# Routing and expert networks in one program block, with lists that carry three numbers for each token

## The chip, the cores and the metric

The kernel runs on one core of one Trainium2 chip. The metric is the device time of one execution in microseconds (us), the median of several runs. The engines are TensorE (PE; its weight loads are PEld), VectorE (DVE), ScalarE (ACT), GpSimd (POOL) and SyncE (SP), which here only issues DMAs. An engine works through its own queue in order; engines wait for each other by semaphores.

## What is computed

A sequence of 16 x 512 tokens with 512 features goes through an attention layer (16 heads, one shared key and value head) and then through a mixture of 16 experts in which each expert picks its 512 tokens. The second half is what the change touches:

```
xn     = xf / rms * norm_weight                      # 8192 tokens x 512
logits = xn @ router_weight.T + router_bias          # 8192 x 16
probs  = softmax(logits)
_, idx = top_k(logits.T, 512)                        # each expert: its 512 best tokens
h      = gelu(xn[idx] @ fc1.T + fc1_bias)            # 2048 hidden
y      = h @ fc2.T + fc2_bias
output = scatter_add(y * gates); divided by the sum of a token's gates
return x + output
```

Matrix products are done in three passes of single precision parts (hi x hi, hi x lo, lo x hi) in the format fp32r.

## The kernel before

It has these stages, each a block of its own, in which every engine has its own program; between two blocks all engines meet.

1. `make_lists`: constants and the list of attention tile pairs.
2. `attend` (0 to about 527 us): a software pipeline over tile pairs. `turn` in each engine's program sets the order of its steps. At the end DVE runs `logits_elsewhere` (L916, L919), which fills in the logits of token tiles that are equal to a common one.
3. A block that clears the 125 semaphores of `attend`, so that their numbers can be used again: SP, POOL, ACT and DVE clear 31 or 32 each.
4. `route` (530 to 616 us): the logits (64 tiles of 128 tokens x 16 experts) are brought into the form 128 rows x 1024, where 8 rows belong to one expert. A search of 16 rounds finds each expert's 512th largest value. In a round ACT and DVE count how many values reach four limits, PE adds the counts, DVE takes the next limits. The softmax is done beside the rounds. Then DVE ranks the chosen tokens (two scans, L1515 and L1518), adds the two kinds of rank (L1528), PE turns the result back to tiles (`b_pos`), and DVE makes from it `pos_f` (the place of each token in each expert's list, L1541), gates divided by their sums (L1548), and two digits of each place, `pos_a` and `pos_b` (L1553 to L1557). SP writes `meta` (gates, and the row of `xn_dram` where the token's features are: 32 numbers, 128 bytes, for each token) to `meta_dram`.
5. `experts` (616 us to the end). For each expert n, DVE builds two sets of flags from the digits (`hot`: `hot_a`, L1908; `named`, L1913 to L1923), PE sums 64 small matmuls into a list of 512 token numbers (`make_list`, L2054, into the PSUM bank `b_turn`), DVE turns that into integers (`name`, L1928 and L1932), POOL moves the list so that it has one number for each partition (`move_list`, L1716), fetches the rows of `meta_dram` (`fetch_meta`, L1722) and with the origin numbers in them the rows of `xn_dram` (`fetch_rows`, L1737). PE turns the rows (L2063), ACT and DVE split them and their sums into hi and lo (`x_hi`, `x_lo`). Then come 8 periods for each expert: 7 products of fc1 in a scheme of Strassen's kind (L2074) and 24 matmuls of fc2 (L272 to L274). POOL makes the weight sums for fc1 (`weight_sums`, L1706 to L1711), ACT and DVE split weights. SP loads weights two buffers ahead. In a loop over the experts the list of expert e+2 and the rows of e+1 are prepared during expert e.

The first expert's list, rows and splits come before the first period, with nothing beside them. In the loop PE takes `make_list` and the transposes between its products, once for each expert.

The lines of the kernel before are L916 and so on as above; `place`, `chosen`, `digits`, `keep_ids`, `first_rows` and `pos_read` are names of the changed kernel.

## Time and profile before

| | us |
|---|---|
| median of 3 runs | 2102.43 (2101.41 to 2103.23) |
| profiled execution, its own time | 2106.12 |
| its span, first to last instruction | 2104.4 |
| attention ends, last logits written (DVE) | 527.0 |
| `route` starts | 530.3 |
| `experts` starts (DVE) | 616.1 |
| first product of the first period (PE) | 657.2 |
| PE busy, share of the span | 1878.0, 89% |

The table follows one execution from left to right. From 657 us on PE works almost without a gap; before that, from 527 us on, it mostly waits. The profile's clock row shows what TensorE was granted in each slice of 52.6 us.

### The profile page before, as it was taken

Reading aid. Unit: us, or ns where it says so; the run is one execution under the profiler, and the core shown is the slowest. Engines: PE = TensorE matmul, PEld = TensorE weight load, DVE = VectorE, ACT = ScalarE, POOL = GpSimd, SP = SyncE. Lnnn points to the kernel's source line nnn. Section 1 sums busy time; section 2 is a strip of 40 time slices with the busy share of each in tenths; the row PEclk is TensorE's granted clock in tenths of the full one; section 3 lists DMA queues with packets and bytes.
Section 4 is the critical chain, followed back from the end, with each engine's and each line's share of the span. In section 5 each row is a group of like instructions: output and inputs, shape, how many; then the busy total and the mean of one; then the engine's idle time right before and its main releaser. Section 6 shows DMA issues by size and latency. Waiting matters only on the chain.

```text
span 2104.4 us, 41265 instructions
## 1 busy us (share of the span) xinstructions
PE 1878.0 (89%) x12264; PEld 1663.4 (79%) x12264; DVE 1569.8 (75%) x2307; ACT 1316.8 (63%) x2618; POOL 1243.9 (59%) x1204
## 2 busy tenths in 40 slices
PE   1788999997115999999999999999999999999996
PEld 1667888885115888898888888898888988899895
DVE  5678888884775777777777777777777777777763
ACT  3656676663514666676666666666666766767663
POOL 1566777764016465856658575675756757567561
PEclk9899999998557999999999999999999999999998
DMA  5765444341932343534434354352543435344351
GB/s 196 233 190 163 110 110 110 111 111 46 299 87 70 122 124 105 146 92 139 116 117 133 101 145 104 121 146 90 145 107 120 135 99 146 99 137 120 116 126 31
DMA packets 96021, 264.04 MB, mean 125 GB/s; under 512 B 20353, under 2 KB 22113, under 8 KB 93025
## 3 DMA queue, kind: packets, MB, share of 16 engines
q1 hardware_dynamic: 78914, 228.74, 34.2%
q0 software_dynamic: 17056, 34.72, 8.9%
q8 instruction: 21, 0.34, 0.1%
q14 instruction: 30, 0.25, 0.0%
HBM read 224.03 MB, written 56.12 MB: 133 GB/s over the span
## 4 chain that ended last, share of the span: by engine, by line
PE 57%; DVE 3%; POOL 3%; issue 3%; DMA 2%; ACT 1%; DVEq 0%; ACTq 0%; POOLq 0%; SPq 0%
PE experts_b_a L2074 15%; PE experts_b_y L272 9%; PE experts_b_y L273 9%; PE experts_b_y L274 9%; PE experts_b_b L2074 8%; PE experts_b_c L2074 4%; PE experts_b_turn L2054 2%; DMA experts_w_raw<-in_w 1%; DVE experts_x_lo L1943 1%; POOL experts_rows L1737 1%; POOL experts_s_raw L1709 1%; PE experts_b_turn L2063 1%; PE experts_b_c L2063 1%; POOL experts_s_raw L1706 0%; DVE experts_w_lo L1994 0%
## 5 line engine op out<-in xcount | busy, mean ns | idle before, releaser
L1706 POOL TENSOR_TENSOR experts_s_raw<-experts_w_raw 128x256 f32<-128x256 f32 x128 | 148.1, 1157 | 509.6 <-DMA experts_w_raw<-in_w 509.0
L272 PE MATMUL experts_b_y<-experts_w_hi,experts_h_hi 128*128 128x512 f32 x1024 | 406.6, 397 | 0.0
L273 PE MATMUL experts_b_y<-experts_w_lo,experts_h_hi 128*128 128x512 f32 x1024 | 403.7, 394 | 0.0
L274 PE MATMUL experts_b_y<-experts_w_hi,experts_h_lo 128*128 128x512 f32 x1024 | 398.7, 389 | 0.0
L2074 PE MATMUL experts_b_a<-experts_x_hi,experts_w_hi 128*128 (+1 forms) x1024 | 292.0, 285 | 9.9 <-DVE experts_x_lo L1937 4.7
L2074 PE MATMUL experts_b_a<-experts_x_hi,experts_w_lo 128*128 (+1 forms) x1024 | 290.4, 284 | 0.0
L2074 PE MATMUL experts_b_a<-experts_x_lo,experts_w_hi 128*128 (+1 forms) x1024 | 290.1, 283 | 0.0
L274 PEld LDWEIGHTS experts_b_y<-experts_w_hi,experts_h_lo 128*128 128x128 f32 x1024 | 192.4, 188 | 43.5
L2074 PEld LDWEIGHTS experts_b_a<-experts_x_hi,experts_w_hi 128*128 128x128 f32 x1024 | 195.0, 190 | 33.8 <-issue 7.7
L272 PEld LDWEIGHTS experts_b_y<-experts_w_hi,experts_h_hi 128*128 128x128 f32 x1024 | 194.3, 190 | 23.7
L273 PEld LDWEIGHTS experts_b_y<-experts_w_lo,experts_h_hi 128*128 128x128 f32 x1024 | 194.4, 190 | 20.9
L2074 PEld LDWEIGHTS experts_b_a<-experts_x_lo,experts_w_hi 128*128 128x128 f32 x1024 | 195.5, 191 | 13.9
L2074 PEld LDWEIGHTS experts_b_a<-experts_x_hi,experts_w_lo 128*128 128x128 f32 x1024 | 195.4, 191 | 0.0
L1902 DVE TENSOR_TENSOR experts_w_lo<-experts_s_raw,experts_w_hi 128x1024 fp32r<-128x1024 f32 x128 | 173.3, 1354 | 2.2 <-ACT experts_w_hi L1794 2.2
L1994 DVE TENSOR_TENSOR experts_w_lo<-experts_w_raw,experts_w_hi 128x1024 fp32r<-128x1024 f32 x128 | 167.8, 1311 | 0.0
L1982 DVE TENSOR_TENSOR experts_h<-experts_p_copy,experts_b_c 128x256 f32<-128x256 f32 x128 | 53.6, 419 | 151.3 <-PE experts_b_c L2074 134.3
L2002 DVE TENSOR_TENSOR experts_h_lo<-experts_h,experts_h_hi 128x512 fp32r<-128x512 f32 x128 | 121.5, 949 | 58.8 <-ACT experts_h_hi L1857 58.7
L1707 POOL TENSOR_TENSOR experts_s_raw<-experts_w_raw 128x256 f32<-128x256 f32 x128 | 162.6, 1270 | 0.0
L2074 PE MATMUL experts_b_b<-experts_x_hi,experts_w_hi 128*128 (+1 forms) x512 | 149.8, 293 | 3.5 <-DVE experts_x_lo L1943 3.5
L1794 ACT ACTIVATE experts_w_hi<-experts_s_raw 128x1024 fp32r<-128x1024 f32 x128 | 134.5, 1051 | 19.9 <-POOL experts_s_raw L1711 19.9
L2074 PE MATMUL experts_b_b<-experts_x_hi,experts_w_lo 128*128 (+1 forms) x512 | 145.0, 283 | 0.0
L2074 PE MATMUL experts_b_b<-experts_x_lo,experts_w_hi 128*128 (+1 forms) x512 | 144.9, 283 | 0.0
(345 smaller groups left out, 5425.4 us busy)
## 6 DMA issues: line engine op xcount, KB each, us to landing
experts_w_raw<-in_w SPq DMA_DIRECT2D x256, 512.0 KB, 3.5
attend_bias<-in_bias SPq DMA_DIRECT2D x68, 256.0 KB, 3.9
attend_spread_w<-weight_dram SPq DMA_DIRECT2D x34, 512.0 KB, 6.6
xn_dram<-g_out_row SPq DMA_DIRECT2D x6, 2304.0 KB, 9.5
attend_q_x<-in_x SPq DMA_DIRECT2D x17, 256.0 KB, 3.6
attend_k_x<-in_x SPq DMA_DIRECT2D x17, 256.0 KB, 5.8
...
```

What stands on the lines that cost most here:

```text
L272: nc.tensor.matmul(out, lh, rh, start=first, stop=False)
L273: nc.tensor.matmul(out, lh, rl, start=False, stop=False)
L274: return nc.tensor.matmul(out, ll, rh, start=False, stop=last)
L1706: nc.gpsimd.tensor_tensor(s1, a21, a22, ALU.add).then_inc(s_done, 1)
L1707: nc.gpsimd.tensor_tensor(s3, a11, a21, ALU.subtract).then_inc(s_done, 1)
L1794: nc.scalar.activation(w1_hi[:, slot, 3:7, :], s_raw[:, slot, :, :], ACT.Copy)\
L1902: nc.vector.tensor_tensor(w1_lo[:, slot, 3:7, :], s_raw[:, slot, :, :], f32(w1_hi[:, slot, 3:7, :]), ALU.subtract).then_inc(w1_lo_done, 1)
L1982: nc.vector.tensor_tensor(h[:, 0, 0:HALF], p1_copy[:, :], b_c[:, 0:HALF], ALU.add)\
L1994: nc.vector.tensor_tensor(w2_lo[:, slot, :], w2_raw[:, slot, :], f32(w2_hi[:, slot, :]), ALU.subtract)\
L2002: nc.vector.tensor_tensor(h_lo[:, slot, 1, :], h[:, 1, :], f32(h_hi[:, slot, 1, :]), ALU.subtract).then_inc(h_lo_done, 1)
L2054: last = nc.tensor.matmul(b_turn[0:16, 0:64], hot_a[:, t, :], named[:, t, :, :].rearrange("p a b -> p (a b)"), start=(t == 0), stop=(t == ...
L2074: last = nc.tensor.matmul(target[:, 0:HALF], left, right, start=first and k == 0 and i == 0, stop=last_in and k == 1 and i == 2, skip_grou ...
```

## The change

`route` and `experts` become one function and one block.

- Weights of the first two chunks, the bias and the copy of x into the output are issued by SP at the start of the block, and POOL sums, ACT splits the first of them during the search (after rounds 8 and 9). DVE splits it after the first expert's flags.
- The ranks of the two kinds are not added on DVE. `flag_g` and `flag_e` stay apart, and PE adds them: 16 fp32r matmuls with an identity accumulate into the two banks, in place of 8 transposes.
- The digits are computed in three DVE operations (`places`, `digits`) for the first expert alone, whose flags and list follow at once. The other experts' digits, the gates and the second list come after.
- A list carries three numbers for each token: SOURCE (the row in `xn_dram`), WEIGHT (the row in `meta_dram`) and TOKEN (the row of the output). So rows are fetched straight from the list, and the gates (now 16 numbers, 64 bytes, for each token) are fetched apart, later. The gates are written by 8 DMAs, after the first expert's rows have been turned.
- Flags have another layout: `hot_a` is [32, 64] in place of [64, 16], `named` is [3, 16, 64] in place of [64, 2, 32]. The tile number is now the innermost index, so each of PE's 64 matmuls reads 48 columns (was 64) that lie 128 bytes apart (were adjacent), and weights of 32 columns (was 16), 128 bytes apart as well.
- The first expert's rows have a semaphore for each quarter, and PE turns each quarter as it lands.
- 74 of the 125 semaphores are cleared, by five engines. `logits_elsewhere` stands later in DVE's last turns.

```diff
@@ attend, DVE's turn
                     if on(-1):
                         query_parts(j - 1, 0)
+                    if edge and not on(-4) and on(-5):
+                        logits_elsewhere(j - 8)
                     if on(-5):
                         out_stats(j - 5)
                     if on(-7):
                         keep_logits(j - 7)
-                    if edge and not on(-3) and on(-4):
-                        logits_elsewhere(j - 7)
@@ clearing
-                for s in counted[3::4]:
+                for s in cleared[3::5]:
                     dve.sem_clear(s)
...
+            @block.tensor
+            def _(pe):
+                for s in cleared[4::5]:
+                    pe.sem_clear(s)
@@ SP
+                load_w1(0, 0)
+                sp.dma_start(b1[:, :, :], io["b1"]).then_inc(b1_in, 16)
+                load_w1(1, 1)
+                load_w2(0, 0)
+                load_w2(1, 1)
+                sp.dma_start(io["out"]..., io["x"]...).then_inc(x_copied, 16)
+                sp.wait_ge(w1_lo_done, 2)
+                load_w1(2, 0)
+                sp.wait_ge(meta_ready, 1)
+                sp.wait_ge(x_turned, KD)
+                for n in range(L):
+                    sp.dma_start(keep["meta_dram"].rearrange("(p t) c -> p t c", t=NT)[:, n * J:(n + 1) * J, :],
+                                 gate[:, :, :].rearrange("p (j l) c -> p l j c", l=L)[:, n, :, :]).then_inc(meta_out, 16)
@@ POOL, first experts
-                weight_sums(0, 0, 0)
-                move_list(0)
-                fetch_meta(0)
-                fetch_rows(0)
-                adopt(0)
-                move_list(1)
-                weight_sums(0, 1, 1)
-                fetch_meta(1)
-                pool.wait_ge(keep["x_copied"], 16)
-                weight_sums(1, 2, 0)
-                weight_sums(1, 3, 1)
+                weight_sums(0, 0, 0)
+                weight_sums(0, 1, 1)
+                move_list(0)
+                fetch_rows(0)
+                fetch_meta(0)          # waits for meta_out, 16 * L
+                keep_ids(0)
+                adopt(0)
+                move_list(1)
+                weight_sums(1, 2, 0)
+                fetch_meta(1)
+                pool.wait_ge(x_copied, 16)
+                weight_sums(1, 3, 1)
                 weight_sums(2, 4, 0)
@@ DVE, after the search
+                nc.vector.scalar_tensor_tensor(flag_g, rank_g, b_gt[:, 0:1], greater, ALU.add, ALU.mult).then_inc(flag_ready, 1)
+                for a in range(2):
+                    nc.vector.scalar_tensor_tensor(flag_e[:, cols], rank_e[:, cols], b_eq[:, 0:1], equal[:, cols],
+                                                   ALU.add, ALU.mult).then_inc(flag_ready, 1)
+                for a in range(2):
+                    dve.wait_ge(pos_turned, a + 1)
+                    step.inc(places(first, a))
+                digits(first)
+                for part in range(4):
+                    hot(0, part)
+                split_w1(0, 0)
+                name(0)
+                for a in range(2):
+                    step.inc(places(others, a))
+                for a in range(2):
+                    chosen(a)
+                dve.sem_inc(pos_read, 1)
+                digits(others)
+                for part in range(4):
+                    hot(1, part)
+                ... row sums, reciprocal, gate * 1/sum -> meta_ready
+                name(1)
@@ DVE, flags
-                        nc.vector.tensor_tensor(hot_a[:, :, :], keep["pos_a"][:, bass.ds(n, 1), :]
-                                                .rearrange("p o t -> p (o t)").unsqueeze(2).to_broadcast([P, NT, 16]),
-                                                keep["ids_a"][:, :].unsqueeze(1).to_broadcast([P, NT, 16]),
+                        nc.vector.tensor_tensor(hot_a[:, :, :], pos_a[:, bass.ds(n, 1), :].to_broadcast([P, LA, NT]),
+                                                ids_a[:, :, :], ALU.is_equal).then_inc(hot_step, 1)
@@ PE
-                        last = nc.tensor.matmul(b_turn[0:16, 0:64], hot_a[:, t, :],
-                                                named[:, t, :, :].rearrange("p a b -> p (a b)"),
+                        last = nc.tensor.matmul(b_turn[0:LA, 0:3 * LB], hot_a[:, :, t],
+                                                named[:, :, :, t].rearrange("p f b -> p (f b)"),
                                                 start=(t == 0), stop=(t == NT - 1))
...
+                pe.wait_ge(list_ready, 3)
+                make_list(1)
+                pe.wait_ge(pos_read, 1)
+                for i, c in enumerate((0, 1, 2, 3)):
+                    pe.wait_ge(first_rows[c], 16)
+                    for k in range(KD):
+                        last = nc.tensor.transpose(b_y[k][...], rows[:, c, k * P:(k + 1) * P], ident)
+                        if c == CT - 1:
+                            last.then_inc(x_turned, 1)
```

How instructions move, on the engines that wait and are waited for. On DVE, in the last turns of the attention: `attend_bias<-logits` and the row below it are `logits_elsewhere`, L766 is the split of the attention output, which PE's last projection reads.

```order
-L916 TENSOR_TENSOR attend_bias<-logits,unseen_tiles 128x1024
-L919 TENSOR_TENSOR logits<-logits,attend_bias 128x1024
 L766 TENSOR_TENSOR attend_oT_lo<-attend_state,attend_oT_hi 128x512 x2
 L885 ISA
 L886 SCALAR_TENSOR_TENSOR attend_xn<-attend_y,attend_y_r,norm_w_row 128x512
+L916 TENSOR_TENSOR attend_bias<-logits,unseen_tiles 128x1024
+L919 TENSOR_TENSOR logits<-logits,attend_bias 128x1024
 L769 BN_STATS attend_o_st<-attend_bank 128x6
```

The two rows now stand behind the split and behind L886.

On DVE, between the ranks and the first flags. Before:

```order
L1537 SCALAR_TENSOR_TENSOR route_gate<-route_b_pos,route_gate 128x512 [waits attend_logits_kept0]
L1541 TENSOR_SCALAR route_pos_f<-route_b_pos 128x8x16 x4
L1544 TENSOR_REDUCE route_row_sum<-route_gate 128x64 [waits attend_xn_turned0]
L1545 TENSOR_SCALAR route_none_sum<-route_row_sum 128x64 [waits attend_xn_turned0]
L1546 TENSOR_TENSOR route_row_sum<-route_row_sum,route_none_sum 128x64 [waits attend_xn_turned0]
L1547 RECIPROCAL route_row_sum<-route_row_sum 128x64 [waits attend_xn_turned0]
L1548 TENSOR_TENSOR route_meta<-route_gate,route_row_sum 128x8x8x16 [waits attend_xn_turned0]
L1553 CAST route_pos_i<-route_pos_f 128x1152
```

And in the changed kernel, from the first expert's digits to its list and the work behind it (`experts_h` holds the places):

```order
L1941 TENSOR_SCALAR experts_pos_a<-experts_h 128x64 [waits attend_biased1,attend_biased2]
L1942 TENSOR_TENSOR experts_pos_b<-experts_h,experts_pos_a 128x64 [waits attend_biased2]
L1703 TENSOR_TENSOR experts_hot_a<-experts_pos_a,experts_ids_a 128x2048 [waits attend_biased2]
L1706 TENSOR_TENSOR experts_named<-experts_pos_b,experts_ids_b 128x1024
L1711 TENSOR_TENSOR experts_named<-experts_named,experts_tile_ids 128x1024 [waits attend_k_turned0]
L1711 TENSOR_TENSOR experts_named<-experts_named,experts_from_ids 128x1024
L1716 TENSOR_SCALAR experts_named<-experts_named,experts_part_id 128x1024 [waits attend_k_turned0]
```

The sums of the gates, and the digits of 18 experts at once, stood ahead of the first flags; now two operations of 64 elements do.

On POOL, from the first list's move to the sums of the chunk that comes next. Before (`ahead_ids` is the moved list; L1706 is the first of a chunk's four sums, here the second chunk's):

```order
L1716 DMA experts_ahead_ids<-experts_list_i 128x1x4 [waits attend_pT_hi_done3]
L1722 DMA experts_rows_meta<-meta_dram,experts_ahead_ids 128x32 [waits attend_pT_hi_done2]
L1722 DMA experts_rows_meta<-meta_dram,experts_ahead_ids 128x32 x3
L1728 COPY experts_rows_id<-experts_rows_meta 128x4 [waits attend_pT_hi_done1]
L1729 COPY experts_next_ids<-experts_ahead_ids 128x4
L1730 COPY experts_next_weight<-experts_rows_meta 128x4
L1737 DMA experts_rows<-xn_dram,experts_rows_id 128x512 [waits attend_pT_turned3]
L1737 DMA experts_rows<-xn_dram,experts_rows_id 128x512 x3
L1743 COPY experts_ids<-experts_next_ids 128x4 [waits attend_pT_turned2]
L1744 COPY experts_weight<-experts_next_weight 128x4
L1716 DMA experts_ahead_ids<-experts_list_i 128x1x4 [waits attend_pT_turned0,attend_pT_turned1,attend_pT_hi_done3]
```

And in the changed kernel. `ahead` is the moved list with its three numbers, L1488 fetches rows, L1477 fetches gates and waits for `meta_out`, and L1458 is the first of the third chunk's sums. The semaphore names in brackets are numbers of `attend` used again:

```order
L1468 DMA experts_ahead<-experts_list_i 128x1x12 [waits attend_qx_hi_done0]
L1488 DMA experts_rows<-xn_dram,experts_ahead 128x512 [waits attend_qx_turned0]
L1488 DMA experts_rows<-xn_dram,experts_ahead 128x512 x3
L1477 DMA experts_rows_meta<-meta_dram,experts_ahead 128x16 [waits attend_qx_turned0,attend_biased3]
L1477 DMA experts_rows_meta<-meta_dram,experts_ahead 128x16 x3
L1493 COPY experts_next_ids<-experts_ahead 128x4
L1496 COPY experts_next_weight<-experts_rows_meta 128x4 [waits attend_kx_done0]
L1502 COPY experts_ids<-experts_next_ids 128x4 [waits attend_y_normed0]
L1503 COPY experts_weight<-experts_next_weight 128x4
L1468 DMA experts_ahead<-experts_list_i 128x1x12 [waits attend_o_root0,attend_o_scale0,attend_qx_hi_done0]
L1458 TENSOR_TENSOR experts_s_raw<-experts_w_raw 128x256 [waits attend_scored0,attend_qT_done1]
```

The fetch of rows now stands ahead of the fetch of gates, and the third chunk's sums stand behind a wait for the write of the gates; the sums of the first two chunks have moved ahead of the first list.

## Rows read from the trace of the kernel before

**Rows 1.** The page: its span, and PE in 40 slices of the span.

```profile
span 2104.4 us, 41265 instructions
...
PE   1788999997115999999999999999999999999996
```

**Rows 2.** Busy time in three stretches: us, engines' busy, clock share, DMA, GB/s.

```profile
530.00:616.00 86.00, 15.71 (x58) 13.40 (x58) 70.79 (x200) 35.91 (x68) 4.20 (x10) 0.50 0.66 207
616.00:657.00 41.00, 10.48 (x144) 9.83 (x144) 21.74 (x23) 7.96 (x9) 26.06 (x28) 0.58 0.32 97
700.00:2070.00 1370.00, 1363.54 (x9318) 1223.29 (x9317) 1036.55 (x1282) 927.09 (x1518) 866.68 (x751) 1.00 0.41 120
```

**Rows 3.** Timeline, DVE then PE, end of attention: start, us, engine, line, operation.

```profile
502.17 1.22 DVE L916 TENSOR_TENSOR attend_bias<-logits,unseen_tiles 128x1024 f32<-128x1024 f32 x1
...
504.69 2.24 DVE L766 TENSOR_TENSOR attend_oT_lo<-attend_state,attend_oT_hi 128x512 fp32r<-128x512 f32 x2
...
507.08 0.76 PE L272 MATMUL attend_bank<-wo_hi,attend_oT_hi 128*128 128x512 f32 x1 [6.31 <-DVE attend_oT_lo L766]
```

**Rows 4.** Timeline of DVE, last logits and first of `route`.

```profile
526.86 0.17 DVE L893 TENSOR_TENSOR logits<-attend_bank,router_b_row 128x16 f32 x1 [3.74 <-PE attend_bank L1071]
...
530.26 0.91 DVE L1473 COPY route_lg<-logits 128x512 f32<-128x512 f32 x2 [3.22 <-PEq L1213]
```

**Rows 5.** Timeline of DVE, from the ranks to the first expert's flags.

```profile
596.84 1.28 DVE L1524 SCALAR_TENSOR_TENSOR route_place_e<-route_rank_e,route_b_eq,route_equal 128x1024 f32<-128x1024 f32 x1
...
600.13 0.69 DVE L1537 SCALAR_TENSOR_TENSOR route_gate<-route_b_pos,route_gate 128x512 f32<-128x512 f32 x1
...
616.06 1.23 DVE L1908 TENSOR_TENSOR experts_hot_a<-pos_a,ids_a 128x1024 bf16<-128x1024 bf16 x1 [5.36 <-PEq L1330]
...
617.21 2.29 DVE L1913 TENSOR_TENSOR experts_named<-pos_b,ids_b 128x2048 bf16<-128x2048 bf16 x1
...
622.35 1.10 DVE L1923 TENSOR_SCALAR experts_named<-experts_named,part_id 128x2048 bf16<-128x2048 bf16 x1
```

**Rows 6.** Timeline of PE: first list, first rows turned, first product.

```profile
623.50 3.58 PE L2054 MATMUL experts_b_turn<-experts_named,experts_hot_a 128*16 128x64 bf16 x64 [22.63 <-DVE experts_named L1923]
...
648.86 3.67 PE L2063 MATMUL experts_b_y<-ident,experts_rows 128*128 128x128 f32 x16 [9.51 <-DMA experts_rows<-xn_dram,experts_rows_id]
...
657.24 0.58 PE L2074 MATMUL experts_b_a<-experts_x_hi,experts_w_hi 128*128 128x256 f32 x1 [4.72 <-DVE experts_x_lo L1937]
```

**Rows 7.** Timeline of POOL: from the first list to the first rows.

```profile
628.25 0.80 POOL L1716 DMA_DIRECT2D experts_ahead_ids<-experts_list_i  x1 [3.42 <-DVE experts_list_i L1932]
...
631.08 2.75 POOL L1722 DMA_INDIRECT experts_rows_meta<-meta_dram,experts_ahead_ids  x1 [2.02 <-DMA experts_ahead_ids<-experts_list_i]
...
640.21 0.19 POOL L1728 COPY experts_rows_id<-experts_rows_meta 128x4 uint32<-128x4 uint32 x1 [1.62 <-DMA experts_rows_meta<-meta_dram,experts_ahead_ids]
...
641.23 0.97 POOL L1737 DMA_INDIRECT experts_rows<-xn_dram,experts_rows_id  x1 [0.59 <-issue]
...
645.01 0.94 POOL L1737 DMA_INDIRECT experts_rows<-xn_dram,experts_rows_id  x1 [0.30 <-issue]
```

**Rows 8.** DVE: strided writes by L1541 (min/median/max ns); contiguous ones (page, part 5).

```profile
L1541 DVE TENSOR_SCALAR route_pos_f<-route_b_pos x8: 361/369/372, 600.7 to 602.9; 128x128 f32<-128x128 f32 x8
...
L1982 DVE TENSOR_TENSOR experts_h<-experts_p_copy,experts_b_c 128x256 f32<-128x256 f32 x128 | 53.6, 419 | 151.3 <-PE experts_b_c L2074 134.3
```

**Rows 9.** Timeline of PE in the loop: a list of 64 matmuls.

```profile
1087.47 2.03 PE L2054 MATMUL experts_b_turn<-experts_named,experts_hot_a 128*16 128x64 bf16 x64
```

**Rows 10.** ACT splits the third chunk's sums; POOL makes them; the write of `meta`.

```profile
671.68 1.05 ACT L1794 ACTIVATE experts_w_hi<-experts_s_raw 128x1024 fp32r<-128x1024 f32 x1
...
655.44 2.32 POOL L1706 TENSOR_TENSOR experts_s_raw<-experts_w_raw 128x256 f32<-128x256 f32 x1
...
661.26 0.73 POOL L1711 TENSOR_TENSOR experts_s_raw<-experts_w_raw,experts_s_raw 128x256 f32<-128x256 f32 x1
...
meta_dram<-route_meta SPq DMA_DIRECT2D x1, 1024.0 KB, 8.7
```

689 lines of the change are left out of this document (331 added, 358 removed).

## The prediction

> **What bounds the kernel now.** I read the page first, then the busy time by stretches, then the timelines of DVE, PE and POOL where PE stands idle. The page gives a span of 2104.4 us, and PE is at nine tenths in nearly all slices but three or four in the middle [rows 1]. The stretches divide this: from 700 to 2070 us PE is busy for 1363.5 of 1370 us at the full granted clock (1.00, 2.4 GHz), so the loop over the experts lasts as long as PE's instructions do, and what DVE, ACT or POOL save there is worth nothing. From 530 to 657 us PE is busy for 26 of 127 us, at a granted share near 0.5 (1.2 GHz), while DVE has 71 of the first 86 us [rows 2]. There the end is set by one chain: DVE's search, ranks and gates, the end of a block, flags, list, a fetch of `meta`, a fetch of rows, the turning. So the change has two places with a price: each us off this chain is a us, and each us that PE's own work in the loop grows is paid 15 times.
>
> The sum is made against the profiled execution: 2106.1 us, of which 2104.4 is the span. The median of the runs is 3.7 us below it, and I take the end result down by that.
>
> **1. End of the attention.** L766 starts right after the two rows of `logits_elsewhere`, at 504.69, and PE waits for it until 507.08 [rows 3]. The two rows move behind L766, into a stretch where DVE waits for PE's projection. Their 504.69 - 502.17 = 2.5 us leave the chain. If PE changes to the full clock at another point, this can be 1 to 4. I take -2.5.
>
> **2. Clearing.** From DVE's last logits, 527.03, to its first work in `route`, 530.26, 3.2 us pass [rows 4], with 31 clears on DVE and two meetings of all engines. 15 clears are left. Were it all clears, 3.2 x 16/31 = 1.7 would go; were it all meetings, nothing. I take -1.1, nearer to the clears, which are most of the instructions there.
>
> **3. Start and search.** The search's instructions are the same. DVE gains one copy (an identity in fp32r), 0.2 us. POOL, idle there before, now sums two chunks beside the first rounds. Where DVE and POOL are both busy, both can stretch: POOL's first fetch, beside flags on DVE, took 2.75 us, its last, beside an idle DVE, 0.94 [rows 7]. ACT's two splits lie in the slack behind rounds 8 and 9. From 0 to +2.5; I take +0.9.
>
> **4. Ranks to the first flags.** Before, the ranks are there at 596.84 + 1.28 = 598.1 and the first flags start at 616.06, 17.9 us later: the addition, gates, four slices of `pos_f` each time, row sums, digits of all experts to 610.70, then 5.36 us of idle time for the write of `meta` and the end of the block [rows 5]. All of it goes behind the first list. Left are PE's fp32r matmuls for the second bank (about 0.8, the turning before took no longer: L1537 starts at 600.13 behind the additions), two reads of 32 places and the two digits with their waits, 0.8. So 1.6 in place of 17.9: -16.3. Bounds: 1.2 to 3.0 left.
>
> **5. Flags, list, integers of the first expert.** From 616.06 to POOL's move of the list at 628.25, 12.2 us [rows 5, 7], of which the flags have 7.4, PE's list and its hand-over 3.7 [rows 6], the integers and the wait of POOL 1.1. The flags shrink from 1024 + 3 x 2048 elements to 2048 + 4 x 1024. At the rate of L1913 (2.29 us for 2048) the four operations with two tensors are 5.7 us and the last at most 0.7: 6.4. At the rate of L1923 (2048 in 1.10, beside POOL) all would be 3.3 [rows 5]. The new operands lie side by side in all tensors, as L1923's do, so I go near the low end: 3.8. The list goes from 64 to 48 columns but with a stride (step 8): 3.4. Two more small operations: +0.3. 8.7 in place of 12.2: -3.5 (-0.5 to -4.5).
>
> The Trainium skill ("VectorE: DVE Perf Modes", What auto-detection actually checks) says that two 16-bit values go through in a cycle when every tensor is 16-bit with step 1. By it the flags would be about 3.4 us, an estimate; the old ones, with one operand of step 0, ran at one per cycle (2.29 us for 2048), with which it agrees.
>
> **6. From the list to the first product.** Before, 628.25 to 657.24, 29.0 us [rows 6, 7]. The fetch of `meta` with its landing and copies (631.08 to 641.23) leaves, 10.15 us. Now: the list lands at +2.8; four fetches of rows take 4.7 (641.23 to 645.95) if DVE is quiet, 7.5 (631.08 to 640.21 - 1.62 = 638.59, the four of `meta`) beside flags; they land 2.9 after the last: +10.4 to +13.2. PE is not free before that: DVE has the others' places, the gates' choice, the digits and the second flags, about 8.6 us from the list, so the second list runs from +7.9 to +11.2. Then 12 transposes (3.67/16 = 0.23 each, 2.8) and the last four, 0.9: turned at about +14.9. Before, 4.7 passed from the last transpose to the first product [rows 6]; now ACT's four copies start later against it, as the last quarter gives all four banks at once: +1.2, so 5.9. Sum 20.8: -8.2 (-4 to -10). This part is nearer to 10 if the second list doesn't delay the transposes.
>
> Together: -2.5 - 1.1 + 0.9 - 16.3 - 3.5 - 8.2 = -30.7.
>
> **7. POOL behind the first rows.** SP writes the gates after the turning, in 8 DMAs of 64-byte pieces, and POOL waits for it ahead of `fetch_meta(0)`; queued behind are the second list's move and the sums of the third chunk, for which ACT waits. With the turning at X: write 8.7 (the old one, of as many pieces) [rows 10], fetch 4.7 to 7.5, landing 1.6, copies and move 1.7, the sums 2.9 (four at 0.73) to 6.5 (655.44 to 661.99): X+19.6 to X+26. ACT took these sums 671.68 - 657.24 = 14.4 after the first product, now X+20.3. The delay is 0 to 6 us; the fourth chunk, with another fetch ahead of it, can add as much. I take +2 (0 to +10). Before, these sums were ready at 662, ten us ahead of ACT.
>
> **8. Lists in the loop.** 15 lists stand in PE's full queue. Each took 2.03 us, 31.7 ns a matmul of 64 adjacent columns [rows 9]. Now there are 48 columns, 128 bytes apart, and 32 weight columns likewise. Low end: only columns count, 48/64 x 2.03 = 1.5, -0.5 x 15 = -7.5. For the stride the trace has only DVE: L1541 wrote 128 strided elements in 369 ns; contiguous results took 419 ns for 256 [rows 8] and 690 for 512 [rows 5], which is 1.06 ns each and 285 ns for 128. The stride added 84/128 = 0.66 ns an element. On PE's 48 columns that is +32 ns: 24 + 32 = 56 ns, 3.6 us a list, +1.5 x 15 = +23. High end: 1.06 + 0.66 = 1.7 ns an element, 82 ns, 5.3 us a list, +3.2 x 15 = +49. The nearest row is the list itself; I take 2.3 us, in which the stride eats somewhat more than the fewer columns give: +0.3 x 15 = +4.5.
>
> DVE's and POOL's changes in the loop (flags on the other layout, rows fetched without waiting for `meta`, three small operations for integers) lie beside PE, which had 6.5 us idle in 1370.
>
> **Forecast.** 2106.1 - 30.7 + 2 + 4.5 = 2081.9, less 3.7: **2078 us**. Its own range is 2064 (low end of 8, part 6 at -10) to 2089.
>
> **Rivals.**
>
> *Strided reads are dear, slower than before.* The 64 matmuls of a list are set by reads at 1.7 ns a column: the high end of 8, +49, and about +2 on the first two lists: 2106.1 - 30.7 + 2 + 51 - 3.7 = 2125. For it speaks DVE's row [rows 8] and that weights and columns are both strided; against it that PE takes in two neighbours faster than DVE takes one, so DVE's price need not be PE's. It decides from 2.03 + 28.7/15 = 3.9 us a list on: beyond that the kernel is slower. Chance 0.20.
>
> The Trainium skill ("SBUF — State Buffer", Specifications (TRN2)) speaks against the change here: lines of 16 bytes, at least two hits in a line for full bandwidth, a penalty at each crossing. Each of the 48 columns is now in a line of its own; the page gives no price for PE.
>
> *The stride costs its addition only.* 3.6 us a list, +23: 2106.1 - 30.7 + 2 + 23 - 3.7 = 2097. Chance 0.18, from 2090 to 2100.
>
> *POOL's backlog lasts.* Part 7 at +10 with the rest as forecast: 2086; the chain is short, but ACT, DVE and PE stand for whole periods at 660 us. For it speaks that POOL's queue holds two fetches and two moves ahead of sums that were early before; against it that POOL is busy for only 867 of 1370 us later [rows 2], so it catches up within a few periods. Chance 0.10.
>
> *It doesn't do what it says.* The flags stay at one element per cycle and the second list holds the transposes up twice as long: +2.6 and +2.6 + 1, 2084. Chance 0.07, within the forecast's range.
>
> **Chances and range.** The forecast has 0.45. Faster by over 0.2% (4.2 us, about what a measurement of this kernel can tell from no change) is below 2098.2: 0.45 + 0.10 + 0.07 and 0.15 of the 0.18: 0.77. Within 0.2%: 0.04. Slower: 0.19. The range for 8 of 10 goes from 2062 to 2114: it holds all but most of the first rival and a little below.
>
> **What would show it.** In the new trace: DVE's first work in the new block at about 526.7 us, the first expert's flags at 597.0, POOL's move of the list at 605.7, the first product at 626.5. Part 8 by the list's row in the loop: 1.5, 2.3, 3.6 or 5.3 us for 64 matmuls. Part 7 by POOL's start on the third chunk's sums against ACT's wait for them, and by the time from the first product to the third period. Part 5 by the new flags' row of 2048 elements, 1.2 or 2.3 us. The forecast is wrong if a list in the loop takes over 3 us, or if the first product isn't at least 25 us earlier.

## The result: slower, 2154.8 us against 2102.8

| | before | changed kernel |
|---|---|---|
| median of 4 runs, us | 2102.83 (2101.41 to 2103.69) | 2154.78 (2151.07 to 2160.33) |
| profiled execution: its time / span, us | 2106.12 / 2104.4 | 2151.07 / 2149.4 |
| mean granted clock of TensorE | 0.952 | 0.943 |

The ratio is 1.025, interval 1.0221 to 1.0279. The profiled execution of the changed kernel was the fastest of its four, so the profiles below differ by 45 us and the medians by 52. The forecast was 2078 with a range from 2062 to 2114, so it was wrong, in sign too. The first rival, "strided reads are dear", had the right direction and 2125.

### The profile page after: what moved, and what is told of

Read it like the earlier page. It is cut to its first block, busy times and chain, and to the rows that moved or that the text cites. A ratio compares the mean times of both kernels' runs of the same rounds, so it can differ in the third digit from the quotient of the medians.

```text
span 2149.4 us, 41315 instructions
## 1 busy us (share of the span) xinstructions
PE 1958.2 (91%) x12272; PEld 1743.5 (81%) x12272; DVE 1504.7 (70%) x2350; ACT 1317.1 (61%) x2618; POOL 1138.7 (53%) x1189
## 4 chain that ended last, share of the span: by engine, by line
PE 68%; DVE 3%; ACT 2%; issue 1%; POOL 0%; DMA 0%; SPq 0%; DVEq 0%; ACTq 0%; POOLq 0%
PE experts_b_a L2035 17%; PE experts_b_y L272 11%; PE experts_b_y L273 11%; PE experts_b_y L274 10%; PE experts_b_b L2035 9%; PE experts_b_turn L2015 4%; PE experts_b_c L2035 4%; ACT experts_h L1647 2%; DVE experts_x_lo L1739 1%; PE experts_b_c L2024 1%; PE experts_b_turn L2024 1%; DVE experts_w_lo L1790 0%; PE experts_b_a L2121 0%; ACT experts_y_out L1599 0%; DVE experts_y_out L1769 0%
## 5 line engine op out<-in xcount | busy, mean ns | idle before, releaser
L272 PE MATMUL experts_b_y<-experts_w_hi,experts_h_hi 128*128 128x512 f32 x1024 | 411.1, 401 | 0.0
L1458 POOL TENSOR_TENSOR experts_s_raw<-experts_w_raw 128x256 f32<-128x256 f32 x128 | 131.8, 1030 | 503.3 <-DMA experts_w_raw<-in_w 502.5
L2035 PEld LDWEIGHTS experts_b_a<-experts_x_hi,experts_w_hi 128*128 128x128 f32 x1024 | 199.9, 195 | 31.0 <-issue 8.2
L2035 PEld LDWEIGHTS experts_b_a<-experts_x_lo,experts_w_hi 128*128 128x128 f32 x1024 | 199.8, 195 | 14.5
L1784 DVE TENSOR_TENSOR experts_h<-experts_u_copy,experts_b_b 128x256 f32<-128x256 f32 x128 | 53.8, 420 | 187.6 <-PE experts_b_b L2035 182.1
L1778 DVE TENSOR_TENSOR experts_h<-experts_p_copy,experts_b_c 128x256 f32<-128x256 f32 x128 | 53.8, 420 | 176.1 <-PE experts_b_c L2035 157.9
L1625 ACT ACTIVATE experts_h<-experts_h,experts_b_now 128x512 f32<-128x512 f32 x128 | 92.3, 721 | 133.2 <-DVE experts_h L1784 130.0
L1798 DVE TENSOR_TENSOR experts_h_lo<-experts_h,experts_h_hi 128x512 fp32r<-128x512 f32 x128 | 117.2, 916 | 77.5 <-ACT experts_h_hi L1636 77.0
L2035 PE MATMUL experts_b_b<-experts_x_hi,experts_w_hi 128*128 (+1 forms) x512 | 154.3, 301 | 3.2 <-DVE experts_x_lo L1739 3.2
```

The lines of the kernel that those rows point to most:

```text
L272: nc.tensor.matmul(out, lh, rh, start=first, stop=False)
L1458: nc.gpsimd.tensor_tensor(s1, a21, a22, ALU.add).then_inc(s_done, 1)
L1625: nc.scalar.activation(h[:, 0, :], h[:, 0, :], ACT.Gelu, bias=b1_now[:, 2 * q:2 * q + 1]).then_inc(gelu_done, 1)
L1778: nc.vector.tensor_tensor(h[:, 0, 0:HALF], p1_copy[:, :], b_c[:, 0:HALF], ALU.add)\
L1784: nc.vector.tensor_tensor(h[:, 0, HALF:CAP], u2_copy[:, :], b_b[:, 0:HALF], ALU.add)\
L1798: nc.vector.tensor_tensor(h_lo[:, slot, 1, :], h[:, 1, :], f32(h_hi[:, slot, 1, :]), ALU.subtract).then_inc(h_lo_done, 1)
```

## The profile after

First the page and the stretch of the loop that answers to [rows 1, 2]:

```profile
span 2149.4 us, 41315 instructions
...
PE   1888999984269999999999999999999999999997
PEclk9899999996569999999999999999999999999998
```

```profile
700.00:2070.00 1370.00, 1364.30 (x8807) 1231.98 (x8805) 936.51 (x1260) 877.77 (x1436) 738.33 (x711) 0.97 0.39 114
```

PE is as busy as before (1364.3 of 1370 us against 1363.5), but it does fewer matmuls in that time (8807 against 9318), and the granted clock is 0.97, where it was 1.00. Busy time alone would have shown nothing: it is the count beside it that tells.

The front half went nearly as forecast. These are the timelines of DVE, PE and POOL in the new kernel (start, us, engine, line, operation), which answer to [rows 3 to 7]:

```profile
500.82 1.22 DVE L916 TENSOR_TENSOR attend_bias<-logits,unseen_tiles 128x1024 f32<-128x1024 f32 x1
...
515.83 0.17 DVE L893 TENSOR_TENSOR logits<-attend_bank,router_b_row 128x16 f32 x1 [3.73 <-PE attend_bank L1071]
518.34 1.68 DVE L1882 COPY experts_rows<-logits 128x512 f32<-128x512 f32 x2 [2.34 <-PEq L1213]
...
520.47 1.93 DVE L1886 CAST experts_h_lo<-ident 128x128 fp32r<-128x128 f32 x1
...
527.01 1.28 DVE L1858 TENSOR_SCALAR_CACHE_REDUCE experts_y_out<-experts_x_raw,experts_limit_hi 128x1024 bf16<-128x1024 int16 x1
...
591.98 1.23 DVE L1703 TENSOR_TENSOR experts_hot_a<-experts_pos_a,experts_ids_a 128x2048 bf16<-128x2048 bf16 x1
593.12 0.69 DVE L1706 TENSOR_TENSOR experts_named<-experts_pos_b,experts_ids_b 128x1024 bf16<-128x1024 bf16 x1
...
595.17 0.48 DVE L1716 TENSOR_SCALAR experts_named<-experts_named,experts_part_id 128x1024 bf16<-128x1024 bf16 x1
...
630.18 0.42 DVE L1778 TENSOR_TENSOR experts_h<-experts_p_copy,experts_b_c 128x256 f32<-128x256 f32 x1 [3.02 <-PE experts_b_c L2035]
```

```profile
595.71 5.72 PE L2015 MATMUL experts_b_turn<-experts_named,experts_hot_a 128*32 128x48 bf16 x64 [4.59 <-DVE experts_named L1716]
610.17 5.69 PE L2015 MATMUL experts_b_turn<-experts_named,experts_hot_a 128*32 128x48 bf16 x64 [8.74 <-DVE experts_named L1716]
615.79 3.68 PE L2152 MATMUL experts_b_y<-ident,experts_rows 128*128 128x128 f32 x16
...
624.52 0.58 PE L2035 MATMUL experts_b_a<-experts_x_hi,experts_w_hi 128*128 128x256 f32 x1 [5.06 <-DVE experts_x_lo L1733]
```

```profile
520.27 1.99 POOL L1524 IOTA experts_ids_a<- 128x2048 bf16 x1
...
602.74 0.81 POOL L1468 DMA_DIRECT2D experts_ahead<-experts_list_i  x1 [71.52 <-DVE experts_list_i L1728]
605.60 1.67 POOL L1488 DMA_INDIRECT experts_rows<-xn_dram,experts_ahead  x1 [2.05 <-DMA experts_ahead<-experts_list_i]
```

The first product is at 624.52, 32.7 us before the old 657.24 [rows 6], and the flags of 2048 elements take 1.23 us, where L1913 needed 2.29 for as many [rows 5]. But each list is a surprise. Here is one of the loop, with PE's products behind it, against [rows 9], and the granted clock in the same stretch (third number from the right):

```profile
1071.92 5.73 PE L2015 MATMUL experts_b_turn<-experts_named,experts_hot_a 128*32 128x48 bf16 x64
...
1077.96 0.41 PE L2035 MATMUL experts_b_b<-experts_x_lo,experts_w_hi 128*128 x1
1078.17 0.41 PE L2035 MATMUL experts_b_b<-experts_x_hi,experts_w_lo 128*128 x1
...
1080.09 0.41 PE L2035 MATMUL experts_b_a<-experts_x_hi,experts_w_lo 128*128 x1
```

```profile
1071.90:1076.00 4.10, 4.10 (x48) 4.08 (x48) 0.00 (x0) 2.17 (x2) 0.41 (x1) 1.00 0.39 128
...
1077.00:1077.60 0.60, 0.60 (x9) 0.46 (x7) 0.00 (x0) 0.00 (x0) 0.60 (x2) 0.50 0.00 0
1077.60:1080.30 2.70, 2.70 (x13) 2.70 (x13) 0.42 (x1) 0.49 (x1) 0.82 (x2) 0.50 0.00 0
1080.30:1082.00 1.70, 1.70 (x10) 1.43 (x10) 1.46 (x2) 1.26 (x3) 0.00 (x0) 0.97 0.00 0
```

Two things are lost. The 64 matmuls take 5.73 us in place of 2.03. And towards their end the granted clock falls to 0.50 (1.2 GHz); the products behind start 0.21 us apart until about 1080.3, and 0.12 apart at 1.00. Note also that the first list, which ran wholly at the half clock (595.71), took 5.72 us: the same. The old list took 3.58 at the half clock and 2.03 at the full one [rows 6, 9]. So the new list takes the same time at either level of TensorE's clock, and the old one did not.

Where the 44.95 us between the two profiled executions are (2151.07 - 2106.12):

| piece, from event to event | before | after | difference |
|---|---|---|---|
| start to the logits ahead of L916, same code | 501.97 | 494.60 | -7.4 |
| from there to DVE's last logits | 24.9 | 21.2 | -3.7 |
| to the first copy of the route | 3.4 | 2.5 | -0.9 |
| to the first rank scan | 60.2 | 62.6 | +2.4 |
| to the first flags | 25.6 | 11.0 | -14.6 |
| to POOL's move of the list | 12.2 | 10.8 | -1.4 |
| to the first product | 29.0 | 21.8 | -7.2 |
| first product to the first sum of `h` | 5.7 | 5.7 | 0 |
| first to last of the 128 sums of `h` (L1982, now L1778) | 1410.9 | 1489.3 | +78.4 |
| the rest | 32.3 | 31.6 | -0.7 |

The first row isn't put down to the change: in the profiles of all kernels below, with the new end of the attention, DVE's last logits lie anywhere from 515.8 to 527.7.

The 128 sums mark the periods. The period with the list lasted 12.7 us in all 15 turns before; now it lasts 17.4 to 19.0, 18.2 in the mean. That is 15 x 5.5 = +82, of which 15 x 3.7 = 55.5 are the matmuls, and 27 are left; the other periods are some 4 us shorter in sum.

That the 27 us are the clock's can be read from the 15 periods themselves, since their matmuls all take 5.73 us and only the stretch of half clock behind the list differs. The shortest of these periods (17.4 us) has 2.3 us of it behind its list, the longest (19.0) has 5.6. In this order:

```profile
890.40:892.70 2.30, 2.30 (x11) 2.30 (x12) 0.42 (x1) 0.14 (x1) 0.81 (x2) 0.50 0.00 0
1549.20:1554.90 5.70, 5.70 (x22) 5.12 (x22) 2.98 (x8) 1.75 (x3) 0.81 (x2) 0.50 0.06 8
```

A straight line through all 15 gives 16.4 us plus 0.46 us for each us of half clock, and misses none by more than 0.12. The 16.4 are what the old period with the slower list would be: 12.7 + 3.7. PE never waits in these two windows, and behind the list of 1071.92 its products start 0.21 us apart in place of 0.12, so a loss of about half of each us is what one would expect.

## The experiments

Each ratio is to the kernel before as timed together with that kernel: 2101.5 us beside e1 to e4, 2102.2 beside e5 to e8, 2099.1 beside e9 to e12. e3, e4, e6 and e7 have one execution each, and what is said of them rests on the list's row, not on their time.

### Which operand's stride it is, e1 to e4

The layout got two sizes, KA for the 32 weight columns and KN for the 48 moving ones: so many tiles lie side by side, and PE steps by that many bf16 values from column to column. 64 is the changed kernel, 1 means adjacent.

```
-        hot_a = sb("hot_a", [P, LA, NT], BF16)
-        named = sb("named", [P, 3, LB, NT], BF16)
+        hot_a = sb("hot_a", [P, NT // KA, LA, KA], BF16)
+        named = sb("named", [P, NT // KN, 3, LB, KN], BF16)
...
-                        last = nc.tensor.matmul(b_turn[0:LA, 0:3 * LB], hot_a[:, :, t],
-                                                named[:, :, :, t].rearrange("p f b -> p (f b)"),
+                        last = nc.tensor.matmul(b_turn[0:LA, 0:3 * LB], hot_a[:, t // KA, :, t % KA],
+                                                named[:, t // KN, :, :, t % KN].rearrange("p f b -> p (f b)"),
```

**e1**, KA = KN = 1. 

> The changed kernel with the flags of a tile side by side again (hot_a 64 tiles x 32, named 64 tiles x 3 x 16). Theory (the stride sets the list, and the slow list drops PE's clock): the 64 matmuls take 1.5 to 2.1 us in the loop instead of 5.73, the granted clock stays 1.00 behind them, DVE's flags go back to 2.3 us for 2048. Loop: 15 x 3.7 = 55 for the lists and about 22 for the clock less than the changed kernel; front: +3 for the first flags, -3 for the first list. Median 2154.8 - 77 = 2078 (2070 to 2085). Rival (32 weight columns in place of 16, or the three products in one bank, not the stride): the list stays over 5 us and the time near 2155.

**e2**, KA = KN = 2. 

> As e1, but the tiles lie in pairs (hot_a 32 x 32 x 2, named 32 x 3 x 16 x 2): PE steps by 4 bytes. Theory (what counts is the distance between a matmul's columns): list between e1's and 5.73; if four columns in 16 bytes are enough for full speed, 1.5 to 2.1 us and a median as e1's, 2078 or, with DVE's flags at two per cycle (1.2 us for 2048), 2075. Rival (any step other than 1 is dear alike): 5.7 us and 2150 to 2155.

**e3**, KA = 64, KN = 1. 

> Changed kernel with only named side by side: the 48 moving columns are adjacent, the 32 weight columns stay 128 bytes apart. If each column read costs alike (89.5 ns / 80 = 1.12 ns): 36 ns for the weights, 24 for the columns: 2.3 us overlapped, 3.8 in a row; if only moving columns cost (1.86 ns each): 1.5 to 2.1 us; if only weights cost (2.8 ns each): 5.7 us. Time 2154.8 less 15 times the list's gain, and less 22 if the clock stays up.

**e4**, KA = 1, KN = 64. 

> Changed kernel with only hot_a side by side: the 32 weight columns are adjacent, the 48 moving columns stay 128 bytes apart. If each column read costs alike: 54 ns: 3.4 us; if only moving columns cost: 5.7 us; if only weights cost: 1.5 to 2.1 us. Time as for e3.

Measured: e1 2089.4 us (2088.0 to 2097.0; ratio to before 0.9953, 0.9935 to 0.9971), e2 2076.1 (2069.5 to 2079.2; 0.9868, 0.984 to 0.9896), e3 2120.8, e4 2162.6. The list in the loop, in this order:

```profile
807.49 1.78 PE L2019 MATMUL experts_b_turn<-experts_named,experts_hot_a 128*32 128x48 bf16 x64
```

```profile
800.15 1.77 PE L2019 MATMUL experts_b_turn<-experts_named,experts_hot_a 128*32 128x48 bf16 x64
```

```profile
704.50 3.82 PE L2019 MATMUL experts_b_turn<-experts_named,experts_hot_a 128*32 128x48 bf16 x64
```

```profile
712.21 5.49 PE L2019 MATMUL experts_b_turn<-experts_named,experts_hot_a 128*32 128x48 bf16 x64
```

So it is the stride, and the rival of e1 (the shapes) falls. With only the weights strided a matmul takes 3.82 / 64 = 59.7 ns, 1.87 ns for each of 32 columns; with only the moving side strided 85.8 ns, 1.79 for each of 48; with both, 89.5 ns, hardly more than the longer side alone. e3 alone would fit the rule that each column costs alike, weights and columns in a row (3.8 us), but that rule gave 3.4 us for e4. None of the three rules that I had put up fits all: either side costs 1.8 to 1.9 ns a strided column, the two are read beside each other, and the longer one counts. In pairs (e2) the stride of 4 bytes is free for PE, and DVE's 2048 flags still take 1.22 us, where e1 needs 2.28.

The times of e1 and e2 are another matter: e1 came out 11 us over its forecast, though its 128 sums take 86 us less than the changed kernel's, where 77 had been forecast. The loss lies ahead of them. Its timelines of POOL and DVE:

```profile
523.59 16.60 POOL L1525 IOTA experts_ids_a<- 128x2048 bf16 x1
540.14 8.91 POOL L1527 IOTA experts_ids_b<- 128x1024 bf16 x1
```

```profile
523.79 16.54 DVE L1890 CAST experts_h_lo<-ident 128x128 fp32r<-128x128 f32 x1
```

The same iota over 2048 values took 1.99 us in the changed kernel, where its innermost run was 64 long; with an innermost run of 1 (and 32 outside it) it takes 16.6, and in e2, with a run of 2, it took 11.77. And a cast on DVE, of 128 x 128, that starts meanwhile lasts until the iota ends. From the first copy to the first round of the search e1 needs 31.0 us, e2 23.5, the changed kernel 8.7, the kernel before 6.8. The Trainium skill ("SBUF — State Buffer", SBUF: two separate sides) says that DVE, in the modes in which it works through two ports, and GpSimd share a pair of ports, which the one that starts first holds for its whole instruction while the other blocks. The two rows agree with it, 16.54 beside 16.60 us; in which mode the cast ran, no row shows.

### The tables made short, e5

```
-                pool.iota(ids_a[:, :, :, :], [[0, NT // KA], [1, LA], [0, KA]], ...
+                pool.iota(ids_a[:, :, :], [[1, LA], [0, KA]], ...
...
-                                                ids_a[:, :, :, :], ALU.is_equal).then_inc(hot_step, 1)
+                                                ids_a[:, :, :].unsqueeze(1).to_broadcast([P, NT // KA, LA, KA]),
+                                                ALU.is_equal).then_inc(hot_step, 1)
```

(`ids_b` likewise; KA = KN = 2.)

> As e2 (tiles in pairs), but POOL's iota makes the two tables of numbers only once per pair (32 x 2 and 16 x 2 values) and DVE reads them broadcast over the pairs. Theory (in e1 to e4 DVE stands in its first casts for as long as POOL's long iota lasts: 16.6 us in e1): from DVE's first copy to the first round 6.8 to 7.2 us in place of e2's 23.5 and the changed kernel's 8.7; the flags of 2048 keep 1.2 us and the list 1.8. Median 2076 - 16.5 = 2059.5 (2055 to 2064). Rival (the broadcast operand puts the flags back to one per cycle): 2.3 us for 2048, +3 on the first list: 2062; rival (DVE waits for something else): no gain on e2, 2076.

Measured 2058.8 us (2053.0 to 2063.4), ratio 0.979 (0.9765 to 0.9816): the forecast of 2059.5 holds. From DVE's first copy to the first round 7.7 us pass (6.8 to 7.2 were expected). In its trace the iota, DVE's cast beside it, the first flags, the first list (at 0.50) and a list of the loop:

```profile
523.22 0.48 POOL L1525 IOTA experts_ids_a<- 128x64 bf16 x1
...
523.41 0.43 DVE L1892 CAST experts_h_lo<-ident 128x128 fp32r<-128x128 f32 x1
...
593.73 1.23 DVE L1707 TENSOR_TENSOR experts_hot_a<-experts_pos_a,experts_ids_a 128x2048 bf16<-128x2048 bf16 x1
...
597.47 2.74 PE L2021 MATMUL experts_b_turn<-experts_named,experts_hot_a 128*32 128x48 bf16 x64 [4.60 <-DVE experts_named L1722]
...
779.81 1.77 PE L2021 MATMUL experts_b_turn<-experts_named,experts_hot_a 128*32 128x48 bf16 x64
```

A broadcast over the pairs, with two adjacent values innermost, leaves DVE's flags at 1.23 us. The period with the list lasts 12.4 us, and, as in e1 and e2, the granted clock of the loop is 1.00 again:

```profile
700.00:2050.00 1350.00, 1336.47 (x9125) 1201.73 (x9123) 987.82 (x1298) 911.29 (x1493) 783.47 (x727) 1.00 0.41 119
```

This kernel beats both. In its profile the first sum of `h` is at 626.20 (before 662.94) and the 128 sums take 1401.4 us (before 1410.9).

### How far apart is dear, e6 and e7

The edit is e5 with one number changed: 4 tiles side by side (8 bytes from column to column), and 8 tiles (16 bytes).

> As e5 with the tiles in fours: PE's columns lie 8 bytes apart, two of them in 16 bytes. Theory A (full speed while two columns lie in 16 bytes): list 1.8 us as in e5, time as e5. Theory B (the cost grows steadily with the distance from 4 bytes on): 2 to 3 us. Theory C (any distance beyond the pairs costs as 128 bytes do): 5.7 us, time e5's + 75.

> As e5 with the tiles in eights: columns 16 bytes apart, each in 16 bytes of its own. Theory A: from here on each column read alone costs 1.8 ns, as at 128 bytes: list 5.7 us, time e5's + 75. Theory B (steady growth with distance): 3 to 4 us, e5's + 20 to 45.

```profile
779.08 3.15 PE L2021 MATMUL experts_b_turn<-experts_named,experts_hot_a 128*32 128x48 bf16 x64
```

```profile
793.63 5.88 PE L2021 MATMUL experts_b_turn<-experts_named,experts_hot_a 128*32 128x48 bf16 x64
```

| bytes from column to column | 2 | 4 | 8 | 16 | 128 |
|---|---|---|---|---|---|
| list of 64, us | 1.78 | 1.77 | 3.15 | 5.88 | 5.73 |
| a matmul / its 48 columns, ns | 0.58 | 0.58 | 1.03 | 1.91 | 1.87 |

Theory A fails for 8 bytes and holds at 16; B fails at 16, C at 8. Two columns in 16 bytes halve the price of one column alone, and four hide it. The times were 2081.3 and 2149.6 us, 22 and 91 above e5. For e6 15 x 1.38 = 21 explains it, without a loss of clock (1.00 from 700 to 2050). For e7 the lists give 15 x 4.11 = 62; its 128 sums take 82 us longer than e5's, at a clock of 0.97, which leaves 20 for the clock, and the rest lies ahead of the first product (628.8 against 620.5).

The rule of 16-byte lines that the prediction had from the Trainium skill ("SBUF — State Buffer", Specifications (TRN2)) points the right way, and at 16 bytes these rows agree; but two hits in a line are not yet full speed for PE's bf16 operands: 3.15 against 1.77 us. The measurement decides.

### The law on the kernel before, e9

Only the layout of the flags is changed in the kernel before (64 moving columns, 16 weights). DVE's operations on them follow the layout and aren't shown:

```
-        hot_a = sb("hot_a", [P, NT, 16], BF16)
-        named = sb("named", [P, NT, 2, 32], BF16)
+        hot_a = sb("hot_a", [P, 16, NT], BF16)
+        named = sb("named", [P, 2, 32, NT], BF16)
...
-                        last = nc.tensor.matmul(b_turn[0:16, 0:64], hot_a[:, t, :],
-                                                named[:, t, :, :].rearrange("p a b -> p (a b)"),
+                        last = nc.tensor.matmul(b_turn[0:16, 0:64], hot_a[:, :, t],
+                                                named[:, :, :, t].rearrange("p a b -> p (a b)"),
```

> The kernel before with nothing changed but the layout of its flags (16 x 64 tiles and 2 x 32 x 64 tiles): PE's 64 moving and 16 weight columns lie 128 bytes apart. Theory (the longer side sets a strided matmul, 1.8 ns a column): 64 x 1.79 to 1.91 = 115 to 122 ns a matmul, a list 7.4 to 7.8 us in place of 2.03, and the clock falls behind it for 2 us or more of loss: 15 x (5.4 to 5.8 + 2 to 3) + 2 x 4 = 119 to 140; median 2220 to 2242. If all 80 columns counted alike (as 89.5 / 80 = 1.12 ns would have it): 89.5 ns, 5.7 us, 2102 + 82 + 4 = 2188.

```profile
822.94 7.22 PE L2053 MATMUL experts_b_turn<-experts_named,experts_hot_a 128*16 128x64 bf16 x64
```

Measured 2201.4 us (2198.8 to 2205.0), ratio 1.0485 (1.0461 to 1.0509), 102 us above the kernel before. 7.22 / 64 = 112.8 ns, 1.76 for each of 64 columns: the longer side sets it, and the rule of 80 equal columns (89.5 ns) falls. The forecast of 2220 to 2242 was too high: the period with the list went from 12.7 to 19.0 to 20.4 us, 19.55 in the mean, so +6.9 a list, of which 5.2 are matmuls and 1.7 are left, not 2 to 3. 15 x 6.9 = 103. The granted clock fell at each of the 15 lists. So the layout alone, with none of the rest of the change, makes the kernel slower, and by 102 us at 64 columns.

### What drops the clock, e8 and e11

**e8**: the changed kernel with each list of the loop cut in four.

```
-                    for t in range(NT):
+                    for t in range(NT) if quarter is None else range(quarter * NT // 4, (quarter + 1) * NT // 4):
...
                     product(b_b, slot, S4, side, B22, False, True)
+                    if more is not None:
+                        more(1)
...
                     product(b_a, slot, S3, side, T3, False, False)
+                    if more is not None:
+                        more(2)
...
                         fc2(*rows, 0, 2)
+                    if more is not None:
+                        more(3)
```

> The changed kernel with each list of the loop cut into four runs of 16 matmuls that stand between products of the same period; columns stay 128 bytes apart. Theory (the slow list is one loss of 3.7 us, the dropped clock behind it another of about 1.4 us a list): the quarters take 1.43 us each, 5.7 together, the granted clock stays 1.00, and the median is 2154.8 - 15 x 1.4 = 2133 (2129 to 2138). Rival (the 1.4 us are a wait that the late list causes on DVE or ACT, or the clock drops anyhow): 2150 to 2160.

Measured 2162.0 us (2150.8 to 2171.5): the forecast of 2133 failed, and no difference from the changed kernel (2151.1 to 2160.3) is shown. Two of the lists, the one of 796.6 and the one of 1081.4, by windows:

```profile
796.60:806.40 9.80, 9.80 (x86) 8.45 (x86) 3.67 (x5) 4.02 (x5) 3.72 (x4) 1.00 0.31 107
1081.40:1087.40 6.00, 6.00 (x59) 5.46 (x59) 1.50 (x3) 4.00 (x5) 2.40 (x4) 1.00 0.27 87
1087.40:1091.40 4.00, 4.00 (x21) 2.83 (x20) 1.86 (x2) 0.00 (x0) 1.31 (x1) 0.57 0.36 131
```

In three of the 15 lists the clock stayed at 1.00, and these three periods took 17.3 us; in the twelve others it fell, and they took 18.4 to 19.3. So the clock's share is seen within one execution, 1.1 to 1.9 us a list. Of the rival, that the time is a wait falls, and that the clock drops anyhow is what came. But cutting the list doesn't keep the clock up, and costs something itself: 17.3 without a loss of clock is 0.9 more than the 16.4 us that e5's 12.4 with 5.73 in place of 1.77 would be. The four runs of 16 take 1.57 us each, 6.3 together, and not 5.7.

**e11**: e5 with each list of the loop done three times over, so as long as the strided one but with adjacent columns.

```
-                    for t in range(NT):
-                        last = nc.tensor.matmul(b_turn[0:LA, 0:3 * LB], ...
+                    for again in range(1 if isinstance(n, int) else 3):
+                      for t in range(NT):
+                        last = nc.tensor.matmul(b_turn[0:LA, 0:3 * LB], ...
```

> As e5, with each list of the loop done three times over (192 matmuls, the first two thirds are thrown away): 5.3 us like the strided list, but at 27.7 ns a matmul. Loss by the list alone: 15 x 3.54 = 53. Theory (the clock falls because the strided matmuls put few columns through per us, not because a list is long): granted clock stays at 1.00, 2058.8 + 53 = 2112. Rival (any 5 us of 48-column matmuls drop it): another 1.8 us a list, 2139.

```profile
791.91 4.97 PE L2022 MATMUL experts_b_turn<-experts_named,experts_hot_a 128*32 128x48 bf16 x192
```

```profile
791.90:796.90 5.00, 5.00 (x194) 4.95 (x193) 0.00 (x0) 2.15 (x2) 1.43 (x3) 1.00 0.30 105
796.90:800.00 3.10, 3.10 (x21) 2.84 (x22) 1.88 (x3) 1.60 (x3) 1.40 (x2) 1.00 0.00 0
```

Measured 2106.9 us (2101.4 to 2117.1) against a forecast of 2112: 48 above e5, as the period with the list went from 12.4 to 15.6 us (15 x 3.2 = 48). The clock stayed at 1.00 behind all 15 lists. 192 adjacent matmuls in 5 us keep it up, 64 strided ones in 5.7 us let it fall, though the profile calls PE busy in both.

These lists of 4.97 us are still 0.8 us shorter than the changed kernel's. e3 closes the gap: its lists have strided weights and take only 3.82 us, and the clock fell at 5 of the 15. Here is one of them, and the stretch behind it:

```profile
1348.30:1352.20 3.90, 3.90 (x66) 3.79 (x65) 0.02 (x1) 2.23 (x2) 0.34 (x1) 1.00 0.39 134
1352.20:1355.80 3.60, 3.60 (x15) 3.41 (x16) 1.24 (x3) 1.53 (x3) 2.48 (x4) 0.53 0.00 0
```

The five periods took 15.8 to 16.0 us, the ten others 14.5. So the length of a list alone does not drop the clock, and the stride does not always: behind strided lists of 3.15 us (e6) it fell in none of 15, of 3.82 in 5, of 5.49 and more (e4, the changed kernel, e7, e9) in all 15. What the chip goes by is not shown.

### POOL's queue and the idle PE, e10 and e12

```
                 fetch_rows(0)
+                weight_sums(1, 2, 0)
                 fetch_meta(0)
                 keep_ids(0)
                 adopt(0)
                 move_list(1)
-                weight_sums(1, 2, 0)
                 fetch_meta(1)
```

> As e5, with POOL's sums of the third chunk ahead of its first fetch of gates. Theory (in e5 ACT waited 1.92 us for these sums and PE's second period took 11.0 us against 10.6 later): the wait goes, 1 to 2 us less than e5's 2058.8. Rival (PE waits at that place for something else, at half the clock): no difference over 0.5 us.

ACT's split of the third chunk's sums, in e5 and then in e10 (with the fourth):

```profile
636.30 1.06 ACT L1574 ACTIVATE experts_w_hi<-experts_s_raw 128x1024 fp32r<-128x1024 f32 x1 [1.92 <-POOL experts_s_raw L1464]
```

```profile
638.64 1.05 ACT L1574 ACTIVATE experts_w_hi<-experts_s_raw 128x1024 fp32r<-128x1024 f32 x1
649.74 1.06 ACT L1574 ACTIVATE experts_w_hi<-experts_s_raw 128x1024 fp32r<-128x1024 f32 x1 [0.45 <-POOL experts_s_raw L1464]
```

Measured 2060.3 us (2057.1 to 2064.2), ratio 0.9814 (0.9794 to 0.9834), no gain on e5. The wait went and the second period fell from 11.0 to 10.5 us, but the third rose from 10.6 to 10.9. A few tenths can't be told from nothing here.

**e12** is e10 with matmuls that nobody reads behind the first list and behind the first rows:

```
+                def filler(times):
+                    for _ in range(times):
+                        nc.tensor.matmul(b_a[:, :], ident_r, flag_g[:, 0:W // 2], start=True, stop=True)
...
                 make_list(0)
+                filler(20)
...
+                filler(9)
                 period(0, 0, 0, 0)
```

> As e10, with 20 matmuls of 512 columns behind the first list and 9 behind the first rows' transposes, whose results nobody reads. In e5 PE stands idle there and runs at 0.50 until 626.8. If work alone brings the clock up: full clock at the second list, the transposes and the first products, 3 to 4 us less than e10. Rival (the clock stays down, or the fillers stand in the way of the transposes): e10's time or up to 3 us more.

```profile
602.00:604.00 2.00, 2.00 (x13) 1.68 (x10) 1.72 (x7) 0.00 (x0) 0.48 (x1) 0.85 0.77 260
604.00:606.00 2.00, 2.00 (x10) 1.65 (x10) 1.82 (x4) 0.00 (x0) 0.34 (x1) 1.00 0.04 5
...
610.00:612.00 2.00, 1.05 (x27) 1.08 (x28) 1.93 (x4) 0.00 (x0) 1.60 (x2) 0.50 0.60 147
```

Measured 2062.7 us (2055.3 to 2065.2): no gain. The work did bring the clock to 1.00, at 602.6, but it was done at 607.2, and by the second list at 610.95 the clock was at 0.50 again; the second set ended at 618.9, and the clock fell again at 623.1, among the first products. One premise was wrong, too: in e5 the clock was at 1.00 from 613.2 to 616.6, at the end of the transposes, without a filler. Fillers that last until the work that they are to help were not tried.

## Why the prediction was wrong

By its own steps:

1. *End of the attention*, -2.5 forecast, -3.7 measured, within its bounds (1 to 4).
2. *Clearing*, -1.1, measured -0.9. Right.
3. *Start and search*, +0.9, measured +2.4, at the edge of the range of 2.5. The reason named (DVE and POOL stretch each other) was right, but the price was in POOL's new iotas and not in its sums: 1.93 us for the identity's cast beside 1.99 of iota. e5, with short tables, has 0.43 for this cast. 1.9 of the 2.4 us lie ahead of the first round of the search (8.7 us from the first copy, 6.8 before).
4. *Ranks to flags*, -16.3, measured -14.7 (588.73, the ranks' end, to 591.98: 3.25 us left and not 1.6). DVE waited for PE's matmuls, 1.58 us and then 0.66: the eight that add the second kind of rank begin only at 589.21 and take 1.91 us at the half clock, where the forecast had 0.8.
5. *Flags and list*, -3.5, measured -1.4. The flags came in at 3.7 us (591.98 to 595.65), forecast 3.8; the list took 5.72 and not 3.4.
6. *List to first product*, -8.2, measured -7.2. The second list, at 5.69 us, stood ahead of the transposes until 615.8; the last fetch had been issued at 611.6.
7. *POOL behind the first rows*, +2: ACT waited 2.03 us for the third chunk and 0.50 for the fourth. Right in kind; e10 shows that it costs no more than a few tenths at the end.
8. *Lists in the loop*, +4.5 forecast, +82 measured in the 15 periods with a list (+78 over all periods). A list took 5.73 us, where the forecast had 2.3 and called itself wrong from 3 on. This is the step that failed, and it is nearly all of the miss: of the 69.2 us between 2081.9 and the profiled execution, 71.2 are the loop, its end and POOL's queue, 5.4 the front, and -7.4 the variation ahead of the change.

In step 8 two things went wrong. The size: 2.3 us were chosen because "the nearest row is the list itself", but that list was an adjacent one and said nothing of a stride. The high end, taken from DVE's L1541 [rows 8], had 1.7 ns a column and 5.3 us a list, only 8% short of 5.73. That it came so near may be luck: L1541 writes fp32 values on DVE, the list reads bf16 values into PE. The middle value, 3.6 us, took the stride as an *addition* to PE's rate on adjacent columns. Measured, strided columns take 1.8 to 1.9 ns each at either level of the clock, while an adjacent list takes 2.74 us at 0.50 and 1.77 at 1.00 (e5). And a term was left out: behind the strided lists the granted clock falls, 27 us in the profiled execution. The forecast priced a list by its own length only. The first rival had the mechanism, but without this second term, so it stopped at 2125.

With the tiles in pairs and short tables of numbers the same change runs in 2059 us (e5), 43 us faster than before and better than the forecast. So the rest of the change does what it was made for, and its layout of flags is what made it slower.
